# The maximum pass of an edge attention layer: one copy for the source terms of four tiles, from a block of twelve row places

## The reference

```
ft = (feat @ W.T).reshape(n, HEADS, OUT_DIM)
a1 = jnp.einsum('nhd,hd->nh', ft, attn_l)
a2 = jnp.einsum('nhd,hd->nh', ft, attn_r)
e = jax.nn.leaky_relu(a1[src] + a2[dst], negative_slope=ALPHA)
m = jax.ops.segment_max(e, dst, num_segments=n)
ex = jnp.exp(e - m[dst])
...
out = jax.ops.segment_sum(msg, dst, num_segments=n)
```

## Time and profile before

| what | value |
|---|---|
| median of three runs (lowest, highest) | 6749.59 us (6747.26, 6761.04) |
| the profiled execution, its own time | 6752.3 us |
| its span, first to last instruction | 6750.5 us |
| mean granted clock of PE over the span | 0.812 |
| the stage `L3Max` in the span | from about 5400 to 6049 us |

### The profile page before, as it was taken

The page is one execution under the profiler, slowest core; times in us unless marked ns, Lnnn a source line. Parts: engine busy times, 40 slices in busy tenths (PEclk is TensorE's granted clock), DMA queues, the critical chain, the costliest instruction groups (busy, mean ns, idle before and its releaser), DMA issues. The chain is left out here.

```text
span 6750.5 us, 92101 instructions
## 1 busy us (share of the span) xinstructions
PE 4675.7 (69%) x21663; PEld 3026.9 (45%) x21663; DVE 3880.6 (57%) x14947; ACT 2148.6 (32%) x7478; POOL 3474.4 (51%) x3739
## 2 busy tenths in 40 slices
PE   3566674747895555638767774778778478888858
PEld 3223333737882222424345553555567233336635
DVE  8676543130016666351578877777532667778875
ACT  0000000212231222302344444444223188874421
POOL 3636665446635666456556663666122166656610
PEclk9776656869996776955689997999788699989978
DMA  1133335546745666013155555777456166664410
GB/s 47 48 98 91 91 92 159 185 143 218 232 149 151 181 181 175 14 45 103 49 151 162 148 145 152 237 237 236 133 150 170 45 173 171 172 154 141 140 44 20
DMA packets 526133, 916.95 MB, mean 136 GB/s; under 512 B 100305, under 2 KB 382880, under 8 KB 517168
## 3 DMA queue, kind: packets, MB, share of 16 engines
q0 software_dynamic: 170800, 477.35, 26.0%
q1 hardware_dynamic: 294378, 305.07, 14.5%
q10 hardware_dynamic: 60438, 128.64, 6.0%
HBM read 739.33 MB, written 171.37 MB: 135 GB/s over the span
## 5 line engine op out<-in xcount | busy, mean ns | idle before, releaser
L999 PE MATMUL bank<-small 128*125 128x256 f32 x1660 | 763.2, 587 | 472.3 <-DVE small L966 239.9
L947 POOL DMA_INDIRECT small<-tabA,idxD x830 | 809.9, 976 | 441.0 <-issue 187.2
L999 PEld LDWEIGHTS bank<-small 128*125 128x125 f32 x1660 | 368.1, 268 | 866.6 <-issue 469.5
L978 DVE TENSOR_TENSOR big<-big,bank 125x256 f32 x830 | 347.1, 418 | 490.4 <-PE bank L999 312.6
L2506 POOL DMA_INDIRECT small<-tabC,idxD x415 | 394.5, 951 | 343.2 <-issue 124.5
L2559 PE MATMUL bank<-small 128*125 128x512 f32 x830 | 474.6, 656 | 127.1 <-issue 104.0
L2548 ACT ACTIVATE small<-cst,small 128x128 f32<-128x128 f32 x1660 | 532.2, 388 | 94.0 <-issue 40.0
L1342 DVE COPY small<-bank 128x256 f32<-128x256 f32 x176 | 74.5, 424 | 834.5 <-PE bank L1382 423.2
L2277 POOL DMA_INDIRECT big<-tabB,idxD x415 | 394.6, 951 | 300.1 <-PE bank L2340 133.6
L2091 POOL DMA_INDIRECT small<-tabT,idxS x415 | 396.5, 955 | 284.5 <-PE bank L1989 141.2
L781 POOL DMA_INDIRECT recs<-pkS,rowS x391 | 383.8, 982 | 249.4 <-issue 100.2
(11 more groups left out here) (463 smaller groups left out, 11371.0 us busy)
## 6 DMA issues: line engine op xcount, KB each, us to landing
small<-eaS SPq DMA_DIRECT2D x830, 128.0 KB
big<-in_L_w ACTq DMA_DIRECT2D x56, 1024.0 KB
eaS<-small SPq DMA_DIRECT2D x415, 128.0 KB
big<-in_L2f_w ACTq DMA_DIRECT2D x64, 512.0 KB
ytab<-small ACTq DMA_DIRECT2D x176, 128.0 KB
big<-rowsS SPq DMA_DIRECT2D x52, 256.0 KB
small<-rowsD SPq DMA_DIRECT2D x52, 256.0 KB
small<-tabA,idxD POOLq DMA_INDIRECT x830
```

The costliest lines, as they stand in the source:

```text
L947: g.indirect_dma_start(out=self.gb[k % self.RG], out_offset=None, in_=K.tabA, in_offset=row_index(K.idxD, k)).then_inc(*self.got.up(k))
L978: v.tensor_tensor(rows, rows, K.bank[k % 4][0:PT, 0:D], ALU.add).then_inc(*self.added.up)
L999: p.matmul(self.K.bank[k % 4][0:PT, 0:D], self.oh[k % self.RO][:, 0:PT], self.gb[k % self.RG], start=True, stop=True).then_inc(*self.summe ...
```

## The change

The eight separate row places become one block `rows` of twelve, of which `gb[i]` is the i-th part. The small copy for each tile goes. After each fourth tile (and after the last) ACT copies the source terms of all tiles of the group with one activation that reads from the block with a stride of 260 numbers: 128 x 16, and 128 x 12 for the last group of three. `spread` is now signalled by the fourth diagonal activation. The group's copy signals a new mark, `taken`, and POOL waits for that one before it reuses a place: the gather of tile k waits for the group of tile k - 12.

```
-    RG = 8
+    RG, CG = 12, 4
...
-        self.gb = [g(AW) for _ in range(self.RG)]
+        self.rows = g(self.RG * AW)
+        self.gb = [self.rows[:, i * AW:(i + 1) * AW] for i in range(self.RG)]
+        self.n_c = (NTE + self.CG - 1) // self.CG
+        self.taken = K.mark(self.n_c)
...
             if k >= self.RG:
                 g.wait_ge(*self.kept_rows.n(k - self.RG))
-                g.wait_ge(*self.spread.n(k - self.RG + 1))
+                g.wait_ge(*self.taken.n((k - self.RG) // self.CG + 1))
...
             for h in range(4):
-                a.activation(self.dg[k % 4][:, h * 128:(h + 1) * 128], K.ident, ACT.Copy, scale=gb[:, D + h:D + h + 1])
-            a.activation(pr.A1[:, 4 * k:4 * k + 4], gb[:, D:AW], ACT.Copy).then_inc(*self.spread.up)
+                m = a.activation(self.dg[k % 4][:, h * 128:(h + 1) * 128], K.ident, ACT.Copy, scale=gb[:, D + h:D + h + 1])
+            m.then_inc(*self.spread.up)
+            if k % self.CG == self.CG - 1 or k == NTE - 1:
+                c, n = k - k % self.CG, k % self.CG + 1
+                at = c % self.RG * AW
+                terms = self.rows[:, at:at + n * AW].rearrange("p (c w) -> p c w", w=AW)[:, :, D:AW]
+                a.activation(pr.A1[:, 4 * c:4 * (c + n)].rearrange("p (c h) -> p c h", h=4), terms, ACT.Copy).then_inc(*self.taken.up)
```

## The result

The change takes 6781.04 us (median of 6 runs, 6772.01 to 6790.16), the kernel before, measured beside it, 6748.08 us (6 runs, 6747.26 to 6761.04). The ratio is 1.0047, with an interval of 1.0034 to 1.0061. I had forecast 6743 us and 6720 to 6758 us, so both the sign and the range were wrong. The profiled execution took 6781.65 us with a span of 6779.8.

What follows compares the result with a forecast made beforehand. PE's own work and pauses were taken to bound the stage, 600 of 645 us, with ACT awaited at 63 of 415 tiles. 4.2 + 1.5 + 0.7 = 6.4 us off 6752.3, with the median 2.7 lower, gave 6743; range 6720 to 6758.

Steps and rivals of the forecast that it cites:

- The sum of ACT's relief: ACT in the stage: small copies removed, 39.4 us, less group copies added, 11.9 us, relieves it of 27.5 us.
- 4.2 us of the relief: Part of ACT's relief reaching the stage, only where PE waits for ACT: 63 tiles x 0.066 us.
- The count of tiles at which PE waits for ACT: Stage tiles whose matmul starts 0.10 us behind ACT's last instruction: 63 of 415 before, fewer expected after.
- `spread` earlier: PE may start 0.095 us earlier at 16 places in the stage where the lead passes from ACT: 1.5 us.
- the tail: End of the stage: gathers start one to four tiles sooner, removing three ACT waits for a gather, 0.7 us.
- Twelve places and the new wait: POOL's gathers in the stage: never later than before, nobody waits for them, so a shorter wait frees nothing.
- ACT sets the stage: Rival: ACT bounds the stage, so the whole 27.5 us relief comes through, 6722 us; chance 0.20.
- POOL becomes the pace: Rival: between pauses ACT follows POOL's 1.25 us a gather, relief at most 5 us, 6745 us; chance 0.06.
- Longer pauses: Rival: up to four more gathers from POOL lengthen PE's 90 idle times, 0.3 us each, 6770 us; chance 0.12.
- more idle time of PE for "issue": Sign of the pauses rival: PE's issue idle time in the stage grows; otherwise it stays near 104 us.
- my own case: The small gain of the sum, 6.4 us, with its own range from 6730 to 6751 us; chance 0.62.
- half-clock stretches: Stage periods with PE at 1.2 GHz; one of 6.8 us costs PE 3.4; two more set the range's slow end.

Runs made afterwards that it cites:

- lead8: The change with POOL also held to a lead of eight tiles, so gathers are let go one by one; 1.0009 to the kernel before where PE pauses.
- e5_before: The kernel before, unchanged, profiled once more in a set with pauses; 6691.14 us.
- e14_change: The change again, unaltered, beside the kernel before in a later set with pauses; 1.0071.
- e10_lead8: The change with POOL also held to a lead of eight tiles, in the set with pauses; median 6701.74 us, 1.0009 to the kernel before.
- early8: The kernel before with `spread` raised by the fourth diagonal, the small copy kept and raising its own mark for POOL, eight places; 1.0002 where PE pauses.
- bunch12: The kernel before with twelve places and POOL held until a group of four is free, ScalarE's instructions untouched; 1.0019.
- e16_pad: The change plus a 4-column ScalarE copy in every tile that nobody reads, now raising `spread`; 6769.18 us, 1.0014 to the kernel before.
- e2_group8: The change with eight places in place of twelve, in the set without pauses; 1.0013 to the kernel before.
- ring12: The kernel before with twelve places in place of eight and nothing else, in a set with pauses; 0.9999.
- ring6: The kernel before with six places in place of eight, in a set with pauses; 1.0004.
- e1_ring12: The kernel before with twelve places in place of eight and nothing else, in the set without pauses; 0.9997.
- e7_ring12: The kernel before with twelve places in place of eight and nothing else, repeated in the set with pauses; 0.9999.

## Why the prediction was wrong

**The sum of ACT's relief: right in size, wrong in use.** Diagonals at 387 ns, the grouped copy at a pace of 0.11 us: as worked out. Where nothing disturbs it ACT now needs 1.195 us a tile (four tiles and their copy from 6039.28 to 6044.06), against the 1.196 of the sum. ACT's busy time fell by 37 us, where I had written 27; I had taken the pace, and the small copy is busy for 190 ns. That 4.2 us of the relief would reach the stage was not seen. lead8 keeps the whole relief and gives places back one by one, and is at 1.0009 (0.9995 to 1.0024). Its gain, if there is one, is below what was measured.

**The count of tiles at which PE waits for ACT went the other way.** I expected fewer than 63. By the same sign (PE 0.10 us behind the fourth diagonal's end) I find 105 in the changed kernel, the last at 6041.81. But the count is no measure of the loss. By the same sign it is 94 in e5_before, the same kernel as the one with 63, 77 in e14_change and 144 in e10_lead8, which loses nothing that can be told. So 63 was a poor base for a forecast, and fewer or more of such tiles says little about the time.

**`spread` earlier and the tail: small, not told apart.** early8 is at 1.0002 (0.9989 to 1.0015), and 1.5 us would be 0.0002 less than 1. ACT waits three times for a gather in place of four, 7.3 us in place of 7.6; I had given 0.7 us for it.

**Twelve places and the new wait: this is the step that failed.** I wrote that the gather of tile k may go "never later" than before, that nobody waits for POOL, and that "a shorter wait frees nothing", and costed the new wait at nothing. The first is true of a single gather, counted in tiles, and none says what four places at a time do. What the runs showed in its place is a loss: 33 us in the first measurement, 50, 44 and 30 in the later sets with pauses, and none that can be told once the same kernel gives its places back one by one (lead8). The 71 stops of POOL of 1.5 us became 19 of 4.4, the longest 7.0, and behind them go four, eight or twelve gathers 1.25 us apart, where before they were mostly seven to nine. bunch12 gives the release in fours without the faster ACT: 13.5 us. I looked at who waits for a gather's data (nearly nobody, then as now) and not at the rhythm of the whole stage.

**And the two parts don't add.** Relief without groups costs nothing that can be told (lead8, in another set), the release in fours alone 0.19%, both 0.71% in the same set as that (intervals 1.0009 to 1.0029 and 1.0048 to 1.0095). My sum treated them as separate terms; the relief was given a value between 0 and 27.5 us and no way to turn into a loss.

**The rivals.** That ACT sets the stage (6722 us, 0.20) is wrong. The Trainium skill, in Perfetto Trace Analysis under Identifying the Most-Contended Engine, takes the engine with the highest occupancy for the bound. Before, that was ACT; the change took 37 us from its busy time and the stage grew by 32, and e16_pad gave it 48 us more and the stage shrank by 21. The trace disagrees with the rule in both directions. That POOL becomes the pace is wrong where PE pauses; in the set without pauses there is a hint of it (in e2_group8 ACT waited 50 times, 29.9 us, for gathers; 1.0013). Longer pauses (6770 us, 0.12) was right in kind and came nearest: but I blamed the four more gathers that POOL may send, which ring12 clears, and I priced it in pauses of PE alone, where 14 of the 32 us were longer matmuls. Its sign failed too: I wanted more idle time of PE for "issue", and that fell from 104.0 to 71.2 us while PE's idle time as a whole grew.

**The range.** Its upper end for my own case, 6751, doesn't follow from its terms: with none of the 4.2 us gained and two half-clock stretches more, 6.8 us, the sum is 6754. The result, 6781.04, lies outside either.

**What stays open.** What holds PE in its pauses, and why one set of runs has them and another hasn't. Whether the long runs of gathers bring the pauses about or only follow them. And how exactly bunches and a fast ScalarE together bring PE to the low clock more often. The timeline above shows a chain that fits (ACT and DVE held twice in a row, PE idle for 5 us, then 6.8 us at half clock, POOL's next gather 7 us late), but it is one place. A longer ring, of sixteen places with groups of four, wasn't run.

None of the variants is shown to beat the kernel before: ring12, early8, lead8 and ring6 are all within 0.1% of it.

## What to carry to other kernels

When a release is made coarser, don't stop at "no single wait gets longer": write down the new rhythm (who stands for how long, how many go at once) and cost that as a part of its own. And write down the old rhythm as well: places that come free one at a time don't mean transfers that go one at a time. Taking work off an engine that isn't the bound isn't free of risk: here it cost 0.5% more once the releases were coarse, and filling the engine up again took some of it back. And where TensorE idles between bursts, put the granted clock into the sum: stage length x (1 - clock) went along here with the loss as no single wait row did. Before calling a count a sign, take it from a second profile of the same kernel: here it was 63 in one and 94 in the other.

## What I had not expected of the hardware

- The same program took 5972 us in one set of runs and 6691 to 6756 us in the others, and the record gives the fast set and one of the slow ones the same chip number, 15. In this stage it was 533 us (e1_ring12) against 643 (the same kernel, e7_ring12), with PE's "issue" waits at 1.1 us against 91.9 and a clock of 0.99 against 0.92.
- How much the granted clock weighs in a stage that looks bound by waits: in the change some 24% of it, 163 us, is at 1.2 GHz (twice the 82 us of the table), against 104 us before (both estimates from the two-digit clock). At the place shown PE had been nearly idle (0.83 us of 5.30) before it fell.
- A ScalarE copy of 128 x 16 with a strided source costs 200 ns, 10 more than one of 128 x 4, and 0.11 us of pace.
